# Adapters mixed by block-diagonal gate matmuls between the steps of layer 0's fill, with a reordered prologue

## What is computed

```python
# cond, one of four convolutions (typ same / upsample / same / downsample)
s = style @ mw.T + mb
weight = SCALE * w * s[:, None, :, None]
demod = rsqrt(sum(weight * weight, axis=(2, 3)) + EPS)
# layer 1's ffn: 16 adapters of rank 32, mixed for each of 8 groups of 4 samples
base_out = matmul(x, kernel) + bias
A_eff = einsum('bn,nri->bri', gate, lora_A)      # gate (8, 16), lora_A (16, 32, 1024)
B_eff = einsum('bn,nor->bor', gate, lora_B)      # lora_B (16, 1024, 32)
delta = B_eff (A_eff x) + lora_B_shared (lora_A_shared x)
```

## Time and profile before

| | |
|---|---|
| median of 3 runs | 2054.01 us (2052.64 to 2054.26) |
| the profiled execution | 2049.0 us, its span 2047.3 us |
| busy: TensorE, VectorE, ScalarE, GpSimd | 1861.4, 904.7, 647.8, 90.5 us |
| mean granted clock of TensorE | 0.947 of full |

### The profile page before, as it was taken

How to read it: one execution, slowest core, us unless ns; L and a number is a source line. 1 busy time by engine, 2 the same in 40 slices (tenths; PEclk the granted TensorE clock), 3 DMA queues, 4 the chain that set the end, 5 groups by cost and what they waited for, 6 DMA issues and landing times.

```text
span 2047.3 us, 28582 instructions
## 1 busy us (share of the span) xinstructions
PE 1861.4 (91%) x9736; PEld 1540.6 (75%) x9736; DVE 904.7 (44%) x2644; ACT 647.8 (32%) x1173; POOL 90.5 (4%) x156
## 2 busy tenths in 40 slices
PE   3789999868999999986799999999978999999995
PEld 2568777757888888865688888888767888888873
DVE  5345555643433434342544444444563343333327
ACT  0035555413333333321522233223143332223310
POOL 0000000000000000000000000000000000002000
PEclk9989999969999999986899999999998999999996
DMA  6255666523232322226322222222143323222217
GB/s 129 56 110 141 161 140 153 131 55 73 78 85 75 84 63 73 74 53 114 81 61 69 59 71 69 59 71 69 33 129 68 80 69 80 63 73 73 69 41 307
DMA packets 248856, 181.29 MB, mean 89 GB/s; under 512 B 198184, under 2 KB 208456, under 8 KB 248814
## 3 DMA queue, kind: packets, MB, share of 16 engines
q1 hardware_dynamic: 242318, 173.36, 33.6%
q0 software_dynamic: 5008, 2.14, 0.9%
q10 hardware_dynamic: 1488, 5.26, 0.8%
HBM read 108.35 MB, written 42.99 MB: 74 GB/s over the span
## 4 chain that ended last, share of the span: by engine, by line
PE 76%; issue 9%; DVE 6%; SPq 4%; DMA 3%; ACT 1%; POOL 0%; DVEq 0%; ACTq 0%; POOLq 0%
PE ps L819 61%; PE ps L1497 4%; PE ps L898 3%; DMA filt<-filt 2%; PE ps L946 2%; SPq L1082 1%; DVE w_lo L1249 1%; SPq L1319 1%; PE ps L889 1%; DMA raw<-in_x 1%; PE ps L1362 1%; PE ps L1368 1%; SPq L1315 1%; DVE filt L655 1%; PE ps L1517 1%
## 5 line engine op out<-in xcount | busy, mean ns | idle before, releaser
L819 PE MATMUL ps<-xp_hi,filt 128*128 128x512 f32 x1024 | 339.2, 413 | 27.7 <-DMA filt<-filt 27.7
L819 PE MATMUL ps<-w_hi,y_hi 128*128 128x512 f32 x768 | 313.5, 408 | 0.0
L819 PE MATMUL ps<-w_hi,y_lo 128*128 128x512 f32 x768 | 306.7, 399 | 0.0
L819 PE MATMUL ps<-w_lo,y_hi 128*128 128x512 f32 x768 | 306.1, 399 | 0.0
L819 PEld LDWEIGHTS ps<-xp_hi,filt 128*128 128x128 f32 x1024 | 192.4, 195 | 71.1 <-DMA filt<-filt 30.1
L644 DVE SCALAR_TENSOR_TENSOR xp_lo<-ps,mods_pair,xp_hi 128x512 fp32r<-128x512 f32 x128 | 96.3, 752 | 267.8 <-ACT xp_hi L394 267.8
L819 PE MATMUL ps<-xp_lo,filt 128*128 128x512 f32 x512 | 205.9, 402 | 0.0
L394 ACT ACTIVATE xp_hi<-ps,mods_pair 128x512 fp32r<-128x512 f32 x128 | 88.4, 690 | 359.2 <-PE ps L819 359.2
L819 PEld LDWEIGHTS ps<-w_lo,y_hi 128*128 128x128 f32 x768 | 146.2, 190 | 35.5
L819 PEld LDWEIGHTS ps<-w_hi,y_hi 128*128 128x128 f32 x768 | 147.6, 192 | 31.5
L407 ACT ACTIVATE y_nat<-ps,mods_pair 128x512 f32<-128x512 f32 x128 | 99.3, 778 | 223.1 <-PE ps L819 223.0
(11 more groups left out here) (317 smaller groups left out, 3149.4 us busy)
## 6 DMA issues: line engine op xcount, KB each, us to landing
x_in<-x_state SPq DMA_DIRECT2D x96, 256.0 KB, 3.9
x_res<-x_state SPq DMA_DIRECT2D x48, 512.0 KB, 3.9
x_state<-x_res SPq DMA_DIRECT2D x46, 512.0 KB, 2.9
filt<-filt SPq DMA_DIRECT2D x128, 128.0 KB, 2.7
filt<-filt SPq DMA_DIRECT2D x128, 96.0 KB, 2.4
raw<-in_x SPq DMA_DIRECT2D x16, 512.0 KB, 5.0
x_res<-in_x SPq DMA_DIRECT2D x16, 512.0 KB, 3.9
x_state<-raw SPq DMA_DIRECT2D x16, 512.0 KB, 3.0
```

The costliest lines, as they stand in the source:

```text
L819: ins = nc.tensor.matmul(out, st[x0], mv[x1], start=first and t == 0, stop=last and t == 2, **kw)
```

## The change

- The mixing: A and B come in by two DMAs (`load_adapters`), with partition (chunk, adapter). The gates are written into a block-diagonal `gate_mat` (128 x 64). A tile is 8 matmuls with the data as stationary and `gate_mat` moving, so nothing is transposed. ScalarE copies the 8 tiles out. Tiles 0 to 3 (A) stand between the steps of pair 0's fill, 4 to 7 (B) around pair 1's halves. The gates load on ScalarE's queue.
- The prologue: squares first, modulation weights transposed and copied ahead of the other forms, copies on ScalarE, clears on GpSimd, x of pair 0 and the adapters ahead of the ffn loads on SyncE's queue, other PSUM banks.
- Layer 0's fill: edge steps stand between the other steps; its ffn transposes and splits come behind mixing, just ahead of the first convolutions.
- All layers: `filter` of pair 1 stands ahead of pair 0's convolutions, x of pairs 1 and 2 is asked for ahead of the filter shifts, and the modulation weights' transposes wait only for the squares.
- Layer 1: shared and bias rows are split once ahead of the fill; the loop splits only the 32 mixed rows, in two halves.

The diff, cut to its core (sizes of buffers, banks and names of semaphores left out):

```diff
         def act_filter(act, l, k, par):
             act.wait_ge(s["pe_k"], pid(l, k) + 1)
+            if not (l == 0 and is_zero(k)):
+                act.wait_ge(s["pe_y"], smp(l, k - 1, 1))
...
+        def dve_prep_sq(dve, l):
+            dve.wait_ge(*cond_loaded(l))
+            link(dve, v.tensor_tensor(wsq_tmp, w_nat[0:C], w_nat[0:C], ALU.mult))
+            v.tensor_reduce(wsq_nat[:].rearrange("p i c -> p (i c)"),
+                            wsq_tmp.rearrange("p i (c k) -> p (i c) k", k=TAPS), AX_X, ALU.add).then_inc(s["sq_forms"], 1)
...
+        def act_prep_modw(act):
+            act.wait_ge(s["modw_T"], 1)
+            copy_modw(act_copy, 0).then_inc(s["modw_out"], 1)
+        def act_prep_conv(act):
+            act.wait_ge(s["cleared"], 1)
+            act.wait_ge(s["forms_T"], 1)
+            copy_conv(act_copy).then_inc(s["forms_hi"], 1)
...
-        DVE_PREP = (dve_prep_forms, dve_prep_transposed, dve_prep_s, dve_prep_var, dve_prep_mods,
-                    dve_prep_bias, dve_prep_bias_out)
+        DVE_PREP = (dve_prep_sq, dve_prep_forms, dve_prep_s, dve_prep_var, dve_prep_mods,
+                    dve_prep_lower, dve_prep_bias, dve_prep_bias_out)
...
-        PE_PREP = (pe_prep_forms, pe_prep_s, pe_prep_norms) + tuple(
+        PE_PREP = (pe_prep_modw, pe_prep_s, pe_prep_norms, pe_prep_conv) + tuple(
...
         def ffn_act_prep(act, l):
...
                 act.wait_ge(s["shared_ready"], 2)
+                nc.scalar.activation(natural(tail_hi[0:65, 0]), tail_raw[0:65, :].rearrange("p (m h) -> p m h", h=2),
+                                     ACT.Copy).then_inc(s["base_act"], 1)
         def ffn_dve_prep(dve, l):
...
+                v.memset(tail_raw[0:32, :], 0.0)
...
                 last.then_inc(s["shared_ready"], 1)
+                dve.wait_ge(s["base_act"], 1)
+                v.tensor_tensor(natural(tail_lo[0:65, 0]), tail_raw[0:65, :].rearrange("p (m h) -> p m h", h=2),
+                                f(natural(tail_hi[0:65, 0])), ALU.subtract).then_inc(s["base_dve"], 1)
...
+        def load_gates(act):
+            for c in range(8):
+                act.dma_start(gate_rep[16 * c:16 * c + 16], w(1, "ffn_gate").rearrange("b n -> n b"),
+                              allow_slow_non_contiguous=True).then_inc(s["gate_loaded"], 16)
+        def load_adapters(sp):
+            sp.dma_start(mix_in[0][:], w(1, "ffn_lora_A").rearrange("n (c r) d -> c n (r d)", c=8)).then_inc(mix_loaded[0], 16)
+            sp.dma_start(mix_in[1][:], w(1, "ffn_lora_B").rearrange("n (c o) r -> c n (o r)", c=8)).then_inc(mix_loaded[1], 16)
...
+        def mix_pe(pe, t):
+            if t == 0:
+                pe.wait_ge(s["gate_ready"], 1)
+            if t % 4 == 0:
+                pe.wait_ge(mix_loaded[t // 4], 16)
+            if t >= 2:
+                pe.wait_ge(s["mix_act"], t - 1)
+            for k in range(8):
+                st = kb_cols(mix_in[0][:, L * t:L * t + L], k) if t < 4 else mix_in[1][:, P * (8 * (t - 4) + k):P * (8 * (t - 4) + k) + P]
+                last = nc.tensor.matmul(ps[:, t % 2, 64 * k:64 * k + 64], st, gate_mat[:].rearrange("p c b -> p (c b)"),
+                                        start=True, stop=True)
...
         def _(sp):
+            sp_load_x(sp, 0, 0)
+            load_adapters(sp)
             ffn_load(sp, 0)
-            sp_load_x(sp, 0, 0)
-            mix_loads(sp)
-            mix_store(sp)
...
+                sp_load_x(sp, l, 1)
                 sp_shift_filter(sp, l, 0)
-                sp_load_x(sp, l, 1)
+                sp_load_x(sp, l, 2)
+                if l == 0:
+                    mix_store(sp)
                 sp_shift_filter(sp, l, 1)
-                sp_load_x(sp, l, 2)
...
         def _(pe):
...
+                if l < 1:
+                    pe_edge(pe, l, 0, 1)
+                    pe.wait_ge(s["dve_e"], edge_count(l, 0, 4))
+                    pe_halves(pe, l, 0)
+                    pe_edge(pe, l, 0, 2)
+                    pe_first(pe, l, 0, 0)
+                    mix_pe(pe, 0)
+                    pe_edge(pe, l, 0, 3)
+                    mix_pe(pe, 1)
+                    pe_first(pe, l, 0, 1)
+                    mix_pe(pe, 2)
+                    pe_edge(pe, l, 0, 4)
+                    mix_pe(pe, 3)
...
                 pe_filter(pe, l, 0)
+                if l == 0:
+                    mix_pe(pe, 4)
                 pe_halves(pe, l, 1)
+                if l == 0:
+                    for t in (5, 6, 7):
+                        mix_pe(pe, t)
+                    pe.wait_ge(s["mix_act"], 8)
...
+                    ffn_pe_prep(pe, 0)
+                pe.wait_ge(s["dve_k"], smp(l, 0, 1))
+                pe_filter(pe, l, 1)
+                if l == 0:
+                    pe.wait_ge(s["raw_dve"], part_count(0, 4))
                 pe_conv(pe, l, 0, 0)
                 pe_conv(pe, l, 0, 1)
                 pe_first(pe, l, 1, 0)
                 pe_first(pe, l, 1, 1)
-                pe_filter(pe, l, 1)
```

More of the change, by code:

```diff
@@ L525, in dve_prep_forms, with copy_modw @@
             last.then_inc(s["conv_forms"], 1)
+        up_T = ps[:, 5, 0:4 * C].rearrange("p (j c) -> p j c", c=C)
+        first_of = [ps[:, 4 + w, 3 * P:4 * P] for w in range(2)]
+        def copy_modw(copy, l):
+            for h in range(2):
+                copy(mod_w_T[:, :, h, :], ps[:, 2, 0:4 * C].rearrange("p (i c) -> p i c", c=C))
+                last = copy(wsq_T[:, :, h, :], ps[0:C, 3, 3 * C:7 * C].rearrange("p (i c) -> p i c", c=C))
+            if l == 0:
+                last = copy(style_T[:], ps[:, 2, 4 * C:4 * C + B])
+            return last
@@ new lines, in copy_conv @@
+        def copy_conv(copy):
+            for h in range(2):
+                copy(first_T[:, :, h, :], ps[0:C, 3, 0:3 * C].rearrange("p (k c) -> p k c", c=C))
+            copy(down_T[:], ps[:, 2, DOWN_COL:DOWN_COL + 3 * C].rearrange("p (k c) -> p k c", c=C))
+            copy(mid_T[:], ps[:, 4, 0:3 * P].rearrange("p (k c) -> p k c", c=P))
+            copy(up_hi[:, 1:5, :], up_T)
+            for w in range(2):
+                last = copy(first_hi[:, w, :], first_of[w])
+            return last
@@ L527, in dve_prep_transposed @@
         def dve_prep_transposed(dve, l):
-            v = nc.vector
+            dve.wait_ge(s["modw_T"], l + 1)
             dve.wait_ge(s["forms_T"], l + 1)
[L532 to L535, removed]
-                v.tensor_copy(style_T[:], ps[:, 2, 4 * C:4 * C + B])
@@ L545, in dve_prep_transposed @@
-            link(dve, last)
-            v.tensor_tensor(up_lo[:, 1:5, :], up, f(up_hi[:, 1:5, :]), ALU.subtract)
-            for w in range(2):
-                v.tensor_tensor(first_lo[:, w, :], first[w], f(first_hi[:, w, :]), ALU.subtract)
-            v.tensor_copy(mid_T[:], ps[:, 4, 0:3 * P].rearrange("p (k c) -> p k c", c=P)).then_inc(s["forms_out"], 1)
+            copy_modw(nc.vector.tensor_copy, l).then_inc(s["modw_out"], 1)
+            copy_conv(nc.vector.tensor_copy).then_inc(s["forms_hi"], 1)
@@ L1760, in _ @@
                              pattern=[[-1, P]], channel_multiplier=1).then_inc(s["ident_ready"], 1)
+            for t in (e_x, e_h, e_z, e_z2):
+                gp.memset(t[:], 0.0)
+            for t in (up_hi, up_lo, end_hi, end_lo):
+                gp.memset(f(t[:]), 0.0)
+            for t in (xp_hi, xp_lo, filt[0], filt[1]):
+                gp.memset(f(t[:]), 0.0)
+            gp.memset(ones[:], 1.0)
+            gp.memset(f(two_ones[:]), 1.0)
+            gp.memset(z_sb[:], 0.0).then_inc(s["cleared"], 1)
             for l in range(LAYERS):
@@ L1806, in _ @@
             dve.sem_inc(s["kernel_dve"], 1)
[L1807 to L1817 removed]
+            dve.wait_ge(s["ident_ready"], 1)
             for l in range(LAYERS):
```

294 lines of the change are left out of this document (156 added, 138 removed).

## The result

The changed kernel takes 2025.67 us (median of 4, 2025.23 to 2026.36) where the kernel before took 2053.32 beside it: a ratio of 0.9874, 95% interval [0.9862, 0.9886]. It is faster by 26 to 28 us; I had forecast 43. Its profiled execution took 2025.23 us, with a span of 2023.5.

The account below looks back on a forecast made before the run. TensorE was taken to bound the loops, so only the prologue and four fills could move. The terms -45.2 - 1.0 + 5.2 - 2.7 + 0.9 = -42.8 us, from 2054.0, gave 2011; range 1999 to 2027.

Parts of the forecast that it names:

- Part A: Prologue up to `mods_ready`: it would come at 30.6 us instead of 39.7, a gain of 9.1.
- Rival 3: Prologue: GpSimd's clears hold VectorE's forms, up to 6.4 us on the chain, total 2017; chance 0.08.
- Part C: Layer 0's fill, `mods_ready` to milestone (pair 1's first convolution): milestone at 87.0 us instead of 132.2.
- rival 2: Layer 0's mixing: the adapters land late, B at 64 us instead of by 50, total about 2022; chance 0.09.
- rival 1: Layer 0's fill: TensorE's clock stays at low level, mixing 14 us more, filters and transposes 3, total 2028; chance 0.12.
- Parts D and F: First step of the loop, gain 1.0 us; three changes of layer, modulation weights' transposes no longer behind `mid_lo`, gain 2.7.
- Part E: Layer 1's fill: a clear and the base rows' split ahead of the mods, loss 5.2 us, bounds 4.5 and 6.
- Part G: Layers 1 to 3: pair 1's filter ahead of the convolutions, +0.3 us a layer, loss 0.9, bounds -2.5 and +4.5.

Follow-up runs that it names:

- e3: The changed kernel with GpSimd's clears issued ahead of its select of the identity; 2026.64 us, 0.9877 of the kernel before.
- e7: e5 with the four large clears moved from GpSimd back to VectorE, in its idle time; 2019.04 us, 0.9838 of the kernel before.
- e1: The changed kernel with the adapters loaded as 16 DMAs of 16 rows in place of two DMAs; 2022.02 us, 0.9866 of the kernel before.
- e5: The changed kernel with partitions ordered (adapter, chunk), so each adapter load is one contiguous run of memory; 2017.46 us, 0.9839 of the kernel before.
- e4: The changed kernel with pair 1's filter back behind the first convolutions in layers 1 to 3; 2020.42 us, 0.9856 of the kernel before.
- e6: The changed kernel with the split of layer 1's base rows moved behind the halves of pair 1; 2022.22 us, 0.9857 of the kernel before.
- e2: The changed kernel with layer 0's small ffn loads ahead of the adapter loads on SyncE's queue; 2035.44 us, 0.9922 of the kernel before.
- e12: e9 with mixing tile 5 moved ahead of the halves of pair 1; 2009.25 us, 0.9799 of the kernel before.
- e10: e9 with 16 spare matmuls in TensorE's idle time of the prologue; 2012.87 us, 0.9819 of the kernel before.
- e9: e5 combined with the changes of e4 and e6, clears left on GpSimd; 2012.98 us, 0.9837 of the kernel before.

## Why the prediction was wrong in size and right in kind

**Part A** put `mods_ready` at 30.6; it came at 31.7. The gates delayed nothing: the weights' first user starts at 7.98, where it started at 8.09. I had taken 1.0, and had counted the pieces wrongly, 1,024 and not 4,096 (8 loads of 128). At 15 ns each they are 1.0 us of all 16 engines and not 3.9, and the turns between two queues, by which I had seen the delay nearer to 3.9, did not show in the time. Rival 3 happened inside this part: GpSimd's clears held VectorE's copy 3.4 us (4.30 against 0.85 in e3). The Trainium skill (SBUF — State Buffer, SBUF: two separate sides) has VectorE and GpSimd lock a port pair for a whole instruction; the trace agrees, with 3.8 us for a copy of 64 columns (0.2 in e3), and it shows the hold through several memsets in a row, to 15.4 us. Without the hold the time would have been below my 30.6; the rest of the sum was a little high. e7 shows the prologue without it, at 28.6. It cost the kernel nothing, for the reason of e3.

**Part C is the step that failed.** It put 56.4 us between `mods_ready` and the milestone; it was 70.5. The sentence that was wrong is that adapters land at 131 GB/s, A at 29 and B at 44. I took the rate for these 4 MB from a window of other transfers. B landed at 56.4; x of pair 1, which I had let be 4 us late, came at 70.05, when ScalarE had stood 10.0 us for it, and tile 7 stood 3.5 us behind ScalarE. That is rival 2, to which I gave 0.09, against which I had set that rows of 16 KB are better than pieces of 128 bytes. The size of the row was not the point. The access pattern was: c n (r d) has 8 as its outermost dimension, and 8 of 16 engines would give the share of 0.52 to 0.55 that the windows show; with 16 rows a DMA or 128 it is 0.93 to 1.07. The engines are only half of it: with all 16 busy the rate rose from 120 to 151 GB/s in e1 and to 316 in e5, where a row took half as long. The Trainium skill (DMA: Bandwidth & Descriptors, Why a DMA increments its semaphore by 16 and not by 1) says that a transfer is dealt to as many engines, up to 16, as divide its slowest dimensions; the traces agree, and had I asked that rule of the diff, I would have given rival 2 far more than 0.09. e5 measures the term: 9.5 us.

The other 4.6 us (60.95 against 56.4) are in my own steps, read from e5: tile 4 ended at 54.6 where I had 52.2 (the first convolution at the lower level took 2.9, not 1.8, and tile 0 2.5); the halves and tiles 5 to 7 took 11.0, I had 10.3 with its 2.5 for the clock; the transposes of layer 0 took 7.04, and I had chosen 4.5 between 3.3 and 7.1 "since TensorE has just been busy". The other steps lay within 0.7. The granted clock was 0.50 from 58 to 78 us in e5, so that is rival 1 in part: not 14 us, since tiles 0 to 4 ran mostly at the upper level (1.9 us each), but the whole stretch behind them did not. Against rival 1 I had set the 1.00 of the earlier trace rows; up to 63.6 us that was no reading. That the measured 2028 is also rival 1's number is chance: of its own 17 us at most 4.6 came.

**Parts D and F**, together 3.7 gained, were 4.2 in the loops and the end. The sum is as forecast; the two can't be told apart, given how much a loop differs between traces. In layer 1 TensorE's wait for `mid_lo` is now followed by the `w_nat` transposes alone.

**Part E** was forecast at 5.2 and is 4.8 by e4, of which e6 gives back 3.9 by moving the two splits.

**Part G** was forecast at 0.9 and is 5.3 by e4, above its bound of 4.5. I costed the order from layer 2's chain alone and let TensorE's convolutions hide the copies; the filter ahead of the convolution delays these, and what they release, in every layer.

The bounds of Part C were added up loosely too: 45.2 less 2.9, 2.6 and 4 is 35.7, not 37. It was 30.1 in the end.

In sum, from span to span: 42.8 forecast, 23.8 measured, and the 19 between them are 9.5 for the loads, 4.6 for the clock and the transposes, 4.4 in Parts E and G and 1.1 in Part A, less 0.5 in D and F. By the ratio the time is 2054.0 x 0.9874 = 2028, one above the end of the range. The range took in most of a slow load by itself and little of a low clock. Both came, each in part, and the later fills with them.

## What to carry to other kernels

Before a rate is taken for a new load, look at its outermost dimension: with 8 there, half of the DMA engines worked, and rows of 16 KB did not help. Then look at the share and the rate together, since a full share was 151 GB/s in e1 and 316 in e5. A queue that is blocked at issue shows a slow transfer ahead of it; moving the blocked ones forward (e2) only moved the wait. And once a fill no longer waits for loads, its time depends on TensorE's clock: try to fill the short waits in its middle with work that is ready (in its one trace, e12 gained 6.6 us by filling a wait of 2.2). Compare several executions before trusting one trace, and read TensorE's level from the durations where the clock has no entry yet.

## What the runs showed of the hardware

- Two loads of 2 MB each, 128 rows of 16 KB: outermost dimension 8, share 0.55 at 120 GB/s; DMAs of 16 rows, 1.00 at 151; one contiguous run, 0.98 at 316 (e1 in that same window: 1.07 at 191). The last two keep all engines busy and still differ up to twofold; a row of 16 KB took 1.7 us in e1 and 0.62 in e5. These runs don't explain it.
- A memset of GpSimd, which reads nothing, kept VectorE out for as long as a row of them lasted (3.8 us for one copy of 64 columns).
- The first select on GpSimd came 8.5 us after the memset ahead of it in the change, 10.9 in e3, 7.6 in e7, and 7.4 before; nothing that the profile shows was waited for.
- TensorE ran at its lower level until the first entry of the clock in each trace: 41.3 us in the change, 63.6 in the kernel before. The time of the rise differs between executions of the same program (41.3 in the change, 50.4 in e6), and with 14 spare matmuls ahead of it, it came at 26.9 in e10's one trace.
- TensorE's fall to 0.50 came at 58.1 in e9, 1.4 us behind the end of a wait of 2.2, and at 65.1 in e12, where that wait was filled.
